# Self- and cross-attention of a decoder layer merged into one program section, with per-batch normalizations on VectorE and GpSimd

## The chip, the cores and the metric

The kernel runs on one core of a Trainium2 chip. The metric is the time of one launch in device microseconds (us), the median of several. TensorE (PE in the rows), VectorE (DVE), ScalarE (ACT), GpSimd (POOL) and SyncE (SP, here only DMA issues) have instruction streams of their own, tied together by semaphores.

## The reference, cut to what matters

B = 8 batches of S = 256 tokens, D = 128, everything in float32. Each sublayer's output is added to its input and normalized without gain or bias.

```python
x = layernorm(x + self_attention(x))             # 16 heads of 8, causal
x = layernorm(x + cross_attention(context, x))   # see below
x = layernorm(x + experts(x))                    # 8 experts of 256, top 2, and a shared one

# cross_attention(context [8, 512, 128], latents = x):
xn, ln = layer_norm(context, g1, b1), layer_norm(latents, g2, b2)
q = ln @ Wq                                      # 16 heads of 64
k, v = split(concatenate([xn, ln]) @ Wkv)        # 768 keys
out = softmax(mask(q k^T / 8)) v @ Wout
```

So the latents are normalized twice between the two attentions: once as the layer's residual, once more with g2 and b2.

## The kernel before, in words

A tile is 128 rows of 128 columns: a batch has 2 tiles of state (`T`), 4 of context (`CT`), together 6 (`KT`). `decoder_layer` calls six stages one after the other, and each is an `nc.Block`, at whose end all engines wait for one another:

```python
self_attention(...)                                 # L311
normalize("n1", ..., whole=True, again=True)        # L207
cross_attention(...)                                # L714
normalize("n2", ...)
experts(...)                                        # L1049
normalize("n3", ..., out=out)
```

**Order of work.** In the attentions and in the experts each engine's stream comes from a table (`Order`, L46): for every kind of step a count per batch and the place of the first, in units of a batch (self-attention 16 heads, cross-attention 32 units of one head and 128 queries, experts 9). A place outside of the batch's own window, such as -4 or 37.75, puts the step among the steps of the batch before or after: the software pipeline. Windows -1, 0, 7 and 8 are written out, windows 1 to 6 are a hardware loop, unrolled by 2 in the attentions (3 turns). `Turns` (L82) deals out PSUM slots in that order and says whose reader has to be done.

**Self-attention**, per batch: projections K, Q, V in three fp32r products (high and low halves); per head POOL makes `q_head` (L469), PE the scores, DVE the masked scores and row minimum (L590), ACT the exponential (L516), PE the transposes (L675), DVE or ACT their copies, PE P times V (L693); per four heads PE spreads the sums (`R`, L701), ACT copies them (L528), DVE divides (`NORM`, L613); at the end PE multiplies by Wo (`OUT`, L708) and DVE adds x. Its step STATS takes bn_stats of the batch's 4 context tiles (L623) and 2 state tiles (L626). SP loads the whole context, 2 MB, into `ctx_all` (L424) near the start, and at about 163 us the experts' weights, 3.3 MB. POOL splits the cross weights into halves (L476, L478).

**n1.** DVE turns the bn_stats of all 48 tiles into mean and 1/sqrt(variance) (a chain of small operations with Sqrt on ACT, table load L289), DVE and ACT normalize the 16 state tiles (L271, L295), DVE takes their bn_stats and goes through the chain a second time.

**Cross-attention**, per batch: DVE normalizes 6 tiles into `normed` (NORMED, L891) and makes the mask rows `bar` (L896); PE transposes (TX for the 2 state tiles, TC for the 4 of context, L976), ACT applies gain and bias into `y` (L839), DVE rounds it to `y_hi` (Y, L901), POOL subtracts to `y_lo` (Y, L819); from these PE makes Q (L990), K (L983) and V; DVE and POOL split K into two halves per head (HI, L907, and LO, L815) and DVE doubles q (TWICE, L921); PE makes scores (S, L1011), DVE masks (L931), ACT takes exponentials (L864, table load at the same line), PE transposes (L1017) and multiplies by V (L1028). Places in the tables of before: TX -26, TC -23 on PE; NORMED -26.75, BAR -26, Y -19 on DVE; Y -25, LO -17.5, WIDE -9.25 on POOL.

**n2, experts, n3.** n2 is as the first half of n1 on the state tiles alone. In the experts the last step of each batch takes bn_stats of the state (L1197); n3 then does the chain (L241 to L258, L289) and the 16 tiles for all batches, and SP issues the output in four transfers of 256 KB (L307).

Of the kernel before, what the change touches and what calls it, by code (L numbers as in the profile page):

```python
# [25 lines left out]
ALU = mybir.AluOpType  # L26
# [19 lines left out]
class Order:  # L46
# [6 lines left out]
    def __init__(self, batches, units, starts):  # L53
        self.batches = batches
        due = []
        for kind, (count, first) in starts.items():
            for i in range(count):
                at = first + i * units / count
                due.append((at % units, kind, int(-(at // units)), i))
        due.sort(key=lambda d: d[0])  # L60
        self.steps = [d[1:] for d in due]
        assert all(-1 <= rel <= 1 for _, rel, _ in self.steps)

    def window(self, w):
        return [s for s in self.steps if 0 <= w + s[1] < self.batches]

    def run(self, engine, emit, unroll):


        def one(w, value):  # L70
            for kind, rel, i in self.window(w):
                emit(kind, value + rel, (w + rel) % 2, i)
        one(-1, -1)
        one(0, 0)
        with engine.Fori(0, (self.batches - 2) // unroll) as turn:
            for n in range(unroll):
                one(1 + n, turn * unroll + 1 + n)
        one(self.batches - 1, self.batches - 1)
        one(self.batches, self.batches)


class Turns:  # L82
# [3 lines left out]
    def __init__(self, order, kinds, places):  # L86
        self.batches, self.places = order.batches, places
# [4 lines left out]
    def place(self, kind, i):  # L92
        return self.at[kind, i] % self.places
# [27 lines left out]
def decoder_layer(nc, x, ctx, mask, wq, wk, wv, wo, g1, b1, g2, b2, xwq, xwkv, xwout,  # L121
# [28 lines left out]
    with top:  # L150
# [9 lines left out]
        stats = sb(top, "stats", [P, B * KT, 6])  # L160
        mean = sb(top, "mean", [P, B * KT])
        rstd = sb(top, "rstd", [P, B * KT])
        var = sb(top, "var", [P, B * KT])
        tmp = sb(top, "tmp", [P, B * KT])
        gb = sb(top, "gb", [P, 4])
        w_rt = sb(top, "w_rt", [P, E])
        w_up = sb(top, "w_up", [P, 2, NE, HID])
        w_down = sb(top, "w_down", [P, NE, HB, D])
# [6 lines left out]
        ctx_all = sb(cross, "ctx_all", [P, B * CT, D])  # L175
# [18 lines left out]
        m.ctx_all, m.keep_all, m.wk_hi, m.wk_lo, m.wv_hi, m.wv_lo = ctx_all, keep_all, wk_hi, wk_lo, wv_hi, wv_lo  # L194
        m.wq_hi, m.wq_lo, m.wout, m.w_up, m.w_down = wq_hi, wq_lo, wout, w_up, w_down
        m.loaded_up, m.loaded_down = sem("loaded_up"), sem("loaded_down")

        self_attention(nc, sem, sb, ps, m)
        normalize(nc, sem, "n1", B * T, state, stats, mean, rstd, var, tmp, T, CT, KT, whole=True, again=True)
        cross_attention(nc, sem, sb, ps, slot, m)  # L200
        normalize(nc, sem, "n2", B * T, state, stats, mean, rstd, var, tmp, T, CT, KT)
        cross.close()
        experts(nc, sem, sb, ps, slot, m)
        normalize(nc, sem, "n3", B * T, state, stats, mean, rstd, var, tmp, T, CT, KT, out=out)


def normalize(nc, sem, name, tiles, state, stats, mean, rstd, var, tmp, T, CT, KT,  # L207
              whole=False, again=False, out=None):
# [8 lines left out]
    stored = sem(name + "_stored")  # L217
    rows = stats[:, :, :].rearrange("p (b k) s -> p b k s", k=KT)

    def per_tile(a, everything):  # L220
        v = a[:, :].rearrange("p (b k) -> p b k", k=KT)
        return v if everything else v[:, :, CT:KT]

    rounds = [whole] + [False] * again
    with nc.Block() as block:  # L225

        @block.vector
        def _(dve):
# [7 lines left out]
            def moments(everything):  # L236

                st = rows if everything else rows[:, :, CT:KT, :]
                me, ve, mo, vo = (st[:, :, :, i] for i in (1, 2, 4, 5))
                m, v, t = (per_tile(a, everything) for a in (mean, var, tmp))  # L240
                link(dve.tensor_tensor(t, me, mo, ALU.subtract))  # L241
                link(dve.tensor_tensor(t, t, t, ALU.mult))  # L242
                link(dve.tensor_tensor(v, ve, vo, ALU.add))  # L243
                link(dve.tensor_scalar(v, v, 1.0 / P, EPS, ALU.mult, ALU.add))  # L244
                link(dve.tensor_scalar(t, t, 0.25, None, ALU.mult))  # L245
                link(dve.tensor_tensor(m, me, mo, ALU.add))  # L246
                link(dve.tensor_scalar(m, m, 0.5, None, ALU.mult))
                dve.tensor_tensor(v, v, t, ALU.add).then_inc(var_ready, 1)  # L248

            def reciprocal_root(n, everything):  # L250

                v, t, r = (per_tile(a, everything) for a in (var, tmp, rstd))
                dve.wait_ge(std_ready, n)
                link(dve.reciprocal(r, r))  # L254
                link(dve.tensor_tensor(t, r, r, ALU.mult))
                link(dve.tensor_tensor(t, t, v, ALU.mult))  # L256
                link(dve.tensor_scalar(t, t, -0.5, 1.5, ALU.mult, ALU.add))  # L257
                link(dve.tensor_tensor(r, r, t, ALU.mult))  # L258

            def at(i):  # L260
                return (i // T) * KT + CT + i % T

            for n, everything in enumerate(rounds):
                moments(everything)
                reciprocal_root(n + 1, everything)
                if n == 0:
                    t, m, r = (per_tile(a, False) for a in (tmp, mean, rstd))
                    dve.scalar_tensor_tensor(out=t, in0=m, scalar=-1.0, in1=r,  # L268
                                             op0=ALU.mult, op1=ALU.mult).then_inc(bias_ready, 1)
                    for i in range(0, tiles, 2):  # L270
                        last = dve.tensor_scalar(state[:, i, :], state[:, i, :], mean[:, at(i):at(i) + 1],  # L271
                                                 rstd[:, at(i):at(i) + 1], ALU.subtract, ALU.mult)
                        if out is not None or i == tiles - 2:
                            last.then_inc(chain, 1)
                            count[0] += 1
                    dve.wait_ge(chain, count[0])
                    if again:
                        for i in range(0, tiles, 2):
                            dve.bn_stats(stats[:, at(i), :], state[:, i, :])
                        for i in range(1, tiles, 2):  # L280
                            dve.wait_ge(act_tiles, i // 2 + 1)
                            last = dve.bn_stats(stats[:, at(i), :], state[:, i, :])
                        link(last)

        @block.scalar
        def _(act):
            for n, everything in enumerate(rounds):
                act.wait_ge(var_ready, n + 1)
# [22 lines left out]
def self_attention(nc, sem, sb, ps, m):  # L311
# [104 lines left out]
    with nc.Block() as block:  # L416

        @block.sync
        def _(sp):
            for i, w in ((0, m.wq), (2, m.wv), (3, m.wo)):  # L420
                sp.dma_start(raw[:, i, :], w).then_inc(loaded_w, 16)
# [845 lines left out]
```

## Time and profile before

| | us |
|---|---|
| median of 3 runs (lowest, highest) | 1204.02 (1203.21, 1204.50) |
| the profiled execution's own time | 1204.94 |
| its span in the trace | 1203.1 |
| PE busy | 1119.0 (93%) |
| DVE busy | 877.1 (73%) |
| ACT busy | 752.6 (63%) |
| POOL busy | 427.4 (36%) |
| mean granted TensorE clock | 0.972 |

The span runs from the first to the last recorded instruction of the profiled execution; that execution's own time is 1.84 us more than its span. Busy times are the sum of an engine's instructions; a granted clock of 1.0 is TensorE's full speed. The self-attention runs from the start to about 199 us, n1 to about 213, the cross-attention to about 985, then n2, the experts to about 1193, and n3.

### The profile page before, as it was taken

To read this page: it belongs to the slowest core of one execution; us is meant where nothing else is said; L and a number is where in the kernel's file an instruction comes from. 1 tells how busy PE (TensorE), PEld (TensorE's weight loads), DVE (VectorE), ACT (ScalarE), POOL (GpSimd) and SP (SyncE) were. 2 spreads that over 40 slices of the span, in tenths; PEclk is the share of its full clock that TensorE was granted. 3 is DMA by queue.
4 is the path that set the end of the run, shared out by engine and by line. 5 is a ranking of instruction groups with operands and counts; after the bars stand their busy time and mean duration, and the time that the engine had idled before them with its cause. 6 is when DMAs were issued, how large, how long until landed. Compare 5 with 4: busy or idle time off the path is not lost. (4 is left out here: it accounts for less than half of the span.)

```text
span 1203.1 us, 29258 instructions
## 1 busy us (share of the span) xinstructions
PE 1119.0 (93%) x8781; PEld 963.3 (80%) x8781; DVE 877.1 (73%) x2772; ACT 752.6 (63%) x1778; POOL 427.4 (36%) x498
## 2 busy tenths in 40 slices
PE   6989894599999999999999989999999986999996
PEld 5777783578888888878888878888888866999995
DVE  7989897687777878767777767777776755555555
ACT  6999895476666767657766666666675754222222
POOL 4656562344435334334433433433433424000000
PEclk9999998799999999999999999999999996899998
DMA  4000050000000000000000000000000000000001
GB/s 141 7 6 9 5 159 1 1 1 2 1 2 2 1 1 2 2 3 2 2 1 2 1 4 2 1 2 1 1 2 1 2 1 1 1 1 0 0 1 35
DMA packets 11403, 12.31 MB, mean 10 GB/s; under 512 B 1152, under 2 KB 9344, under 8 KB 11136
## 3 DMA queue, kind: packets, MB, share of 16 engines
q1 hardware_dynamic: 10848, 10.43, 2.9%
q8 instruction: 67, 1.10, 0.4%
q14 instruction: 72, 0.59, 0.2%
q10 hardware_dynamic: 416, 0.20, 0.1%
HBM read 9.57 MB, written 1.05 MB: 9 GB/s over the span
## 5 line engine op out<-in xcount | busy, mean ns | idle before, releaser
L815 POOL TENSOR_TENSOR xk_parts<-k_raw,xk_parts 64x768 fp32r<-64x768 f32 x128 | 236.4, 1847 | 441.1 <-DVE xk_parts L907 441.1
L931 DVE CUSTOM_DVE_ANT_0 xmasked<-ps,bar 128x768 f32<-128x768 f32 x256 | 244.0, 953 | 6.0 <-issue 1.6
L864 ACT ACTIVATE xprobs<-xmasked,xlow 128x768 f32<-128x768 f32 x256 | 237.9, 929 | 4.6 <-issue 3.8
L1011 PE MATMUL ps<-xk_parts,xq_parts 128*128 128x512 f32 (+1 forms) x1024 | 232.2, 348 | 4.7 <-DVE xq_parts L912 2.9
L1017 PE MATMUL ps<-ident,xprobs 128*128 128x128 f32 x1536 | 215.5, 276 | 2.0 <-DVE xprobs_t L936 1.1
L1011 PEld LDWEIGHTS ps<-xk_parts,xq_parts 128*128 128x128 f32 x1024 | 174.5, 189 | 28.8 <-DVE xq_parts L912 3.4
L1028 PE MATMUL ps<-xprobs_t,xvals 128*64 128x256 f32 x1536 | 179.9, 383 | 1.1 <-ACT xprobs_t L870 1.1
L1017 PEld LDWEIGHTS ps<-ident,xprobs 128*128 128x128 f32 x1536 | 169.4, 140 | 10.7 <-DVE xprobs_t L936 1.3
L1028 PEld LDWEIGHTS ps<-xprobs_t,xvals 128*64 128x64 f32 x1536 | 104.9, 137 | 57.8 <-issue 10.4
L936 DVE COPY xprobs_t<-ps 128x768 f32<-128x768 f32 x128 | 121.6, 950 | 4.7 <-PE ps L1017 4.5
L112 DVE MEMSET xspare<- 128x1 f32 x256 | 15.1, 59 | 145.4 <-PE ps L1011 110.9
L1128 ACT ACTIVATE silu<-ps 128x512 f32<-128x512 f32 x72 | 42.8, 597 | 123.0 <-PE ps L1230 123.0
L516 ACT ACTIVATE probs<-masked,low 128x128 f32<-128x128 f32 (+1 forms) x256 | 114.0, 453 | 2.6 <-DVE low L590 2.5
L870 ACT ACTIVATE xprobs_t<-ps 128x768 f32<-128x768 f32 x128 | 103.3, 807 | 4.1 <-PE ps L1017 2.6
L1180 DVE TENSOR_TENSOR hidden<-ps,silu 128x512 f32<-128x512 f32 x72 | 49.6, 691 | 75.6 <-ACT silu L1128 75.6
L844 ACT ACTIVATE k_raw<-ps 128x768 f32<-128x768 f32 x64 | 52.0, 812 | 74.2 <-PE ps L985 71.1
L1228 PE MATMUL ps<-cxt_hi,up_hi 128*128 (+1 forms) x288 | 88.7, 308 | 0.0
L469 POOL TENSOR_TENSOR q_head<-q_parts,head_of 128x256 fp32r<-128x256 f32 x128 | 76.1, 614 | 31.7 <-DVE q_parts L580 30.9
L876 ACT ACTIVATE xrsum_t<-ps 128x256 f32<-128x256 f32 x64 | 24.6, 384 | 99.4 <-PE ps L1036 99.4
L1230 PE MATMUL ps<-cxt_hi,up_lo 128*128 (+1 forms) x288 | 83.3, 289 | 0.0
L1229 PE MATMUL ps<-cxt_lo,up_hi 128*128 (+1 forms) x288 | 83.1, 288 | 0.0
L1236 PE MATMUL ps<-w_down,hidden 128*128 128x128 f32 x576 | 77.1, 278 | 4.2 <-DVE hidden L1180 4.2
(182 smaller groups left out, 2391.1 us busy)
## 6 DMA issues: line engine op xcount, KB each, us to landing
w_up<-in_L_ffn_w SPq DMA_DIRECT2D x2, 1024.0 KB, 8.8
raw_kv<-in_L_xattn_Wkv SPq DMA_DIRECT2D x1, 1024.0 KB, 11.7
out<-state SPq DMA_DIRECT2D x4, 256.0 KB, 2.6
x_in<-in_x SPq DMA_DIRECT2D x7, 128.0 KB, 2.2
raw_q<-in_L_xattn_Wq SPq DMA_DIRECT2D x1, 512.0 KB, 7.7
wout<-in_L_xattn_Wout SPq DMA_DIRECT2D x1, 512.0 KB, 3.8
keep_all<-in_mask_BxS_bk SPq DMA_DIRECT2D x1, 512.0 KB, 5.7
w_up<-in_L_ffn_sw SPq DMA_DIRECT2D x2, 128.0 KB, 6.9
```

The source lines that it names most:

```text
L516: nc.scalar.activation(probs[:, i % 4, lo:hi], masked[:, r, lo:hi], ACT.Exp, scale=-1.0, bias=low[:, r, j:j + 1], accum_out=sums[:, g % 2, ...
L815: pool.tensor_tensor(k_parts[dst, i // 2 % 2, h, :], k_raw[src, :], k_parts[src, i // 2 % 2, h, :].bitcast(F32), ALU.subtract).then_inc(k_ ...
L864: nc.scalar.activation(probs[:, i % 4, :], masked[:, i % 4, :], ACT.Exp, scale=-1.0, bias=low[:, i % 4:i % 4 + 1], accum_out=sums[:, pair ...
L870: nc.scalar.activation(probs_t[:, i % 4, :, 0, :], slot(slots.place("PT", 2 * i), KEYS).rearrange("p (k t) -> p k t", k=KT), ACT.Copy).the ...
L931: dve.tensor_tensor_reduce(masked[:, i % 4, :], slot(slots.place("S", i), KEYS), bar[:, par, :], 1.0, 3e38, ALU.add, ALU.min, low[:, i % 4 ...
L936: dve.tensor_copy(probs_t[:, i % 4, :, 1, :], slot(slots.place("PT", 2 * i + 1), KEYS).rearrange("p (k t) -> p k t", k=KT)).then_inc(pt_dv ...
L1011: last = nc.tensor.matmul(slot(s, hi - lo, lo), q_parts[:, pair % 2, h, part, t * P:(t + 1) * P], k_parts[:, pair % 2, h, lo:hi], start=pa ...
L1017: last = nc.tensor.transpose(slot(s, P, j * P), probs[:, i % 4, j * P:(j + 1) * P], ident[:, :])
L1028: last = nc.tensor.matmul(ps[h * XD:(h + 1) * XD, O_BANK + i % 2, 0:S], vals[:, i // 2 % 2, j, c:c + XD], probs_t[:, (2 * i + h) % 4, j, : ...
L1228: nc.tensor.matmul(o, wh, xh, start=True, stop=False)
L1229: nc.tensor.matmul(o, wh, xl, start=False, stop=False)
L1230: last = nc.tensor.matmul(o, wl, xh, start=False, stop=True)
```

## The change

1. Both attentions stand in one `nc.Block`. `self_attention` and `cross_attention` now return emit functions per engine. `Order.run` takes `between`, steps of the cross-attention's first batch to be inserted at given places of the self-attention's last windows, and `done`, the kinds not to be issued again; `apart=2` lets the self-attention's loop cover windows 1 to 4 only (2 turns) and writes out 5 and 6.
2. n1 is gone. Per batch the cross-attention does it itself: DVE STATS (6 bn_stats), POOL N1 (12 operations on 128x2, the inverse root by `ALU.pow` and one Newton step, seven waits on its own results), DVE NORM1 (normalizes the 2 state tiles, bn_stats of the result), POOL N2 (the same 12 on 128x6), DVE NORMED one tile at a time. STATS leaves the self-attention but for batch 0.
3. The context comes per batch (256 KB) into a double buffer, the first two loads near the start, the others once `normed` of two batches before is done. The experts' weights are loaded once the self-attention's last batch is added, and memory is laid out anew.
4. n3 is gone: in the experts POOL does the 12 operations per batch, DVE normalizes at place 9 + 2 + 2.25 units, and SP stores each batch (128 KB).
5. n2 stays, without its options.

```diff
-    def run(self, engine, emit, unroll):
+    def run(self, engine, emit, unroll, between=None, done=(), apart=0):
...
-        with engine.Fori(0, (self.batches - 2) // unroll) as turn:
+        with engine.Fori(0, (self.batches - 2 - apart) // unroll) as turn:
             for n in range(unroll):
                 one(1 + n, turn * unroll + 1 + n)
-        one(self.batches - 1, self.batches - 1)
-        one(self.batches, self.batches)
+        for w in range(self.batches - 1 - apart, self.batches + 1):
+            one(w, w)
...
+            @block.gpsimd
+            def _(pool):
+                emit = c.gpsimd(pool)
+                a.gpsimd(pool, {B - 1: steps(emit, "N1", 5, 0, 1) + steps(emit, "N2", 5, 9, 1),
+                                B: steps(emit, "Y", 1, 9, 1)})
+                c.pool_order.run(pool, emit, 2, done=("N1", "N2", "Y"))
...
+                a.scalar(act, {B: steps(emit, "TX", 1, 5, 1) + steps(emit, "TC", 1, 5, 1)})
...
+                a.vector(dve, {B - 2: steps(emit, "STATS", KT, 0, 2),
+                               B - 1: steps(emit, "NORM1", 2, 4, 1) + steps(emit, "NORMED", KT, 13, 0.5),
+                               B: steps(emit, "BAR", 1, 3, 1) + steps(emit, "Y", 1, 7, 1)})
...
+                a.tensor(pe, {B: steps(emit, "TX", 1, 4, 1) + steps(emit, "TC", 1, 4, 1)})
...
         "R": (PAIRS, 5.25), "PV": (PAIRS, 5), "PT": (UNITS, 0.75), "OUT": (1, 37.75),
-        "TC": (1, -23), "TX": (1, -26)})
+        "TC": (1, -13), "TX": (1, -14.5)})
...
-        "NORM": (PAIRS, 9.25), "PT": (UNITS // 2, 2.25), "OUT": (1, 38.5), "NORMED": (1, -26.75),
-        "BAR": (1, -26), "Y": (1, -19), "TWICE": (XH, -5)})
+        "NORM": (PAIRS, 9.25), "PT": (UNITS // 2, 2.25), "OUT": (1, 38.5), "NORMED": (KT, -17.5, 0.5),
+        "BAR": (1, -26), "Y": (1, -11), "TWICE": (XH, -5),
+        "STATS": (KT, -32, 0.75), "NORM1": (2, -23.5, 0.75)})
...
-        "LO": (XH, -17.5), "WIDE": (PAIRS, -9.25), "Y": (1, -25)})
+        "LO": (XH, -5.5), "WIDE": (PAIRS, 2.75), "Y": (1, -13), "N1": (5, -30.5, 1), "N2": (5, -24.5, 1)})
...
+            if group == 2:
+                pool.wait_ge(link, b * LINKS + 3)
+                pool.tensor_tensor(root, var, half, ALU.pow).then_inc(link, 1)
...
+            if kind == "NORM1" and i == 0:
+                dve.wait_ge(scaled1, b + 1)
...
+            if kind == "NORM1" and i == 1:
+                dve.wait_ge(half_renewed, T * (b + 1))
+                dve.memset(early.spare[:, :], 0.0)
...
+                    dve.wait_ge(scaled2, b + 1)
...
+                if kind == "Y" and i == NE - 1:
+                    wait(dve, scaled, b)
+                if kind == "NORM":
+                    dve.wait_ge(scaled, b + 1)
```

**How the order moves.** First PE, from the end of the self-attention's last window to the cross-attention's first Q; `heads_t` and `wo_t` are the self-attention's, `y_hi` the cross-attention's. Before:

```order
L675 MATMUL ps<-ident,probs 128x128 x6
L693 MATMUL ps<-probs_t,vals 32x256 x4
L693 MATMUL ps<-probs_t,vals 32x128 x4
L701 MATMUL ps<-ident,rsum_wide 128x128 x2
L708 MATMUL ps<-wo_t,heads_t 128x128 x8
L416 UNCONDITIONAL_BRANCH
L963 UNCONDITIONAL_BRANCH
L976 MATMUL ps<-ident,normed 128x128 x6
L990 MATMUL ps<-y_hi,wq_hi 128x256
```

And now:

```order
L647 MATMUL ps<-ident,probs 128x128 x6
L1043 MATMUL ps<-ident,normed 128x128 x6
L665 MATMUL ps<-probs_t,vals 32x256 x4
L665 MATMUL ps<-probs_t,vals 32x128 x4
L673 MATMUL ps<-ident,rsum_wide 128x128 x2
L680 MATMUL ps<-wo_t,heads_t 128x128 x8
L1060 MATMUL ps<-y_hi,wq_hi 128x256
```

The two branches, the block's end and the next one's start, are gone, and the transposes of `normed` stand ahead of the last P times V. DVE now, in the same window:

```order
L578 COPY probs_t<-ps 128x384 x2
L587 RECIPROCAL rsum<-sums 128x8
L594 TENSOR_TENSOR heads_t<-ps,rsum_t 128x256
L959 MEMSET bar 128x2x256
L961 TENSOR_SCALAR bar<-keep_all 128x512
L578 COPY probs_t<-ps 128x384
L594 TENSOR_TENSOR heads_t<-ps,rsum_t 128x256
L966 CAST y_hi<-y 128x768
L598 TENSOR_TENSOR state<-ps,x_in 128x256
```

Two mask operations stand ahead of the last copy of transposed probabilities, and the rounding of `y` ahead of the last addition. Third, POOL now, in the window before that one, where nothing stood between `q_head`, `rsum_wide` and the weight splits:

```order
L814 TENSOR_TENSOR x_gap<-xstats 128x6
L815 TENSOR_TENSOR x_var<-xstats 128x6
L816 TENSOR_TENSOR x_total<-xstats 128x6
L452 TENSOR_TENSOR q_head<-q_parts,head_of 128x256
L819 TENSOR_TENSOR x_fix<-x_gap 128x6
L820 TENSOR_SCALAR x_var<-x_var 128x6
L821 TENSOR_SCALAR x_mean<-x_total 128x6
L823 TENSOR_TENSOR x_var<-x_var,x_fix 128x6
L452 TENSOR_TENSOR q_head<-q_parts,head_of 128x256
L467 TENSOR_TENSOR rsum_wide<-ones,rsum 128x256
L826 TENSOR_TENSOR x_root<-x_var,x_powers 128x6
```

The chain N2 now lies between the `q_head` of the last batch, on which PE's scores wait; N1 lies the same way ahead of it. In the cross-attention the same two chains lie between the LO steps.

## Rows read from the trace of the kernel before

**Rows 1.** Windows: start:end, length, each engine's busy (x instructions), PEclk, DMA share, GB/s
```profile
162.77:184.41 21.64, 20.97 (x202) 17.63 (x201) 20.58 (x117) 21.08 (x86) 13.86 (x26) 1.00 0.69 214
210.00:230.00 20.00, 9.26 (x40) 7.87 (x41) 10.01 (x33) 4.92 (x10) 5.62 (x3) 0.63 0.00 1
400.00:600.00 200.00, 197.11 (x1471) 164.93 (x1468) 150.71 (x388) 132.54 (x253) 77.91 (x68) 0.99 0.01 2
1100.00:1160.00 60.00, 60.00 (x518) 60.00 (x517) 32.49 (x84) 15.53 (x26) 0.00 (x0) 1.00 0.00 0
```
**Rows 2.** Timeline, self-attention: start us, us, engine line, out<-in xcount [idle before <-releaser]
```profile
47.43 0.38 ACT L528 ACTIVATE rsum_t<-ps 128x256 f32<-128x256 f32 x1 [0.36 <-PE ps L701]
...
69.27 0.38 ACT L528 ACTIVATE rsum_t<-ps 128x256 f32<-128x256 f32 x1 [0.36 <-PE ps L701]
...
81.74 0.06 DVE L112 MEMSET spare<- 128x1 f32 x1 [3.03 <-issue]
...
93.91 0.38 ACT L528 ACTIVATE rsum_t<-ps 128x256 f32<-128x256 f32 x1 [0.36 <-PE ps L701]
...
140.93 0.39 ACT L528 ACTIVATE rsum_t<-ps 128x256 f32<-128x256 f32 x1 [0.36 <-PE ps L701]
```
**Rows 3.** Timeline, the context half of one batch's STATS on DVE
```profile
186.76 0.86 DVE L623 BATCH_NORM_STATS2 stats<-ctx_all 128x6 f32<-128x128 f32 x4
```
**Rows 4.** Timeline, from the self-attention's end to the first Q
```profile
196.61 2.02 PE L708 MATMUL ps<-wo_t,heads_t 128*128 128x128 f32 x16 [1.02 <-DVE heads_t L613]
...
213.50 0.48 DVE L881 MEMSET bar<- 128x512 f32 x1 [0.67 <-PEq L225]
...
213.90 0.93 DVE L891 TENSOR_SCALAR normed<-ctx_all,mean,rstd 128x128 f32<-128x128 f32 x4
...
214.74 0.59 DVE L891 TENSOR_SCALAR normed<-state,mean,rstd 128x128 f32<-128x128 f32 x2
...
215.25 0.42 DVE L896 TENSOR_SCALAR bar<-keep_all 128x512 f32<-128x512 uint8 x1
...
216.12 0.56 ACT L839 ACTIVATE y<-ps,gb 128x256 f32<-128x256 f32 x1 [4.42 <-PE ps L976]
...
217.78 0.56 DVE L901 CAST y_hi<-y 128x768 fp32r<-128x768 f32 x1 [2.11 <-ACT y L839]
...
218.42 1.80 POOL L819 TENSOR_TENSOR y_lo<-y,y_hi 128x768 fp32r<-128x768 f32 x1 [24.36 <-DVE y_hi L901]
...
220.37 0.55 PE L990 MATMUL ps<-y_hi,wq_hi 128*128 128x256 f32 x1 [3.43 <-POOL y_lo L819]
```
**Rows 5.** Timeline, the filling of the cross-attention
```profile
221.14 0.63 PE L983 MATMUL ps<-y_hi,wk_hi 128*128 128x512 f32 x1
...
227.15 0.96 PE L1011 MATMUL ps<-xk_parts,xq_parts 128*128 128x512 f32 x4 [1.70 <-DVE xq_parts L912]
...
227.95 0.40 PE L983 MATMUL ps<-y_hi,wk_hi 128*128 128x512 f32 x1
...
230.49 1.28 ACT L864 ACT_TABLE_LOAD   x1
```
**Rows 6.** Groups by line: POOL's LO, count, busy us, mean ns, idle before
```profile
L815 POOL TENSOR_TENSOR xk_parts<-k_raw,xk_parts 64x768 fp32r<-64x768 f32 x128 | 236.4, 1847 | 441.1 <-DVE xk_parts L907 441.1
```
**Rows 7.** By source line: count, ns min/median/max, first and last start, forms
```profile
L921 DVE CAST xq_parts<-xq_parts x128: 419/422/1349, 222.7 to 969.0; 64x512 fp32r<-64x512 f32 x128
...
L469 POOL TENSOR_TENSOR q_head<-q_parts,head_of x128: 612/614/620, 11.4 to 186.1; 128x256 fp32r<-128x256 f32 x128
...
L826 POOL TENSOR_TENSOR xrsum_wide<-ones,xrsum x128: 392/401/623, 243.6 to 986.2; 128x128 f32<-128x128 f32 x128
...
L1103 POOL MEMSET index<- x8: 127/128/134, 1004.4 to 1004.7; 128x16 f32 x8
```
**Rows 8.** Timeline, the end
```profile
1192.53 0.49 DVE L1197 BATCH_NORM_STATS2 stats<-state 128x6 f32<-128x128 f32 x2
...
1197.60 2.67 SPq L307 DMA_DIRECT2D out<-state  x4
```

More of the change, by code:

```diff
@@ L92, in place @@
     def place(self, kind, i):
-        return self.at[kind, i] % self.places
+        return (self.at[kind, i] + self.shift) % self.places
     def before(self, kind, batch, i):
@@ L199, in decoder_layer @@
[L199 to L202, printed above, removed]
+        m.loaded_rest, m.loaded_ctx = sem("loaded_rest"), sem("loaded_ctx")
+        m.cross_hi, m.cross_lo = sem("cross_hi"), sem("cross_lo")
+        m.self_added = sem("self_added")
+        early = cross_early(cross, sb, m)
@@ L216, in normalize @@
     act_tiles = sem(name + "_act_tiles")
[L217 to L224, printed above, removed]
+    me, ve, mo, vo = (stats[:, :, i] for i in (1, 2, 4, 5))
+    m, v, t, r = (a[:, :] for a in (mean, var, tmp, rstd))
     with nc.Block() as block:
@@ L234, in link @@
                 dve.wait_ge(chain, count[0])
[L236 to L248, printed above, removed]
@@ L263, in _ @@
[L263 to L283, printed above, removed]
@@ L298, in normalize @@
-        if out is not None:
-            @block.sync
-            def _(sp):
-                rows_out = out.rearrange("b (j p) d -> p (b j) d", p=P)
-                step = 2 * T
-                for i in range(0, tiles, step):
-                    sp.wait_ge(chain, 12 + (i + step) // 2)
-                    sp.wait_ge(act_tiles, (i + step) // 2)
-                    sp.dma_start(rows_out[:, i:i + step, :], state[:, i:i + step, :]).then_inc(stored, 16)
-                sp.wait_ge(stored, 16 * (tiles // step))
@@ L311, in self_attention @@
-def self_attention(nc, sem, sb, ps, m):
+            act.wait_ge(var_ready, 1)
+            nc.scalar.activation(r, v, ACT.Sqrt).then_inc(std_ready, 1)
+            act.wait_ge(bias_ready, 1)
+            for i in range(1, tiles, 2):
+                nc.scalar.activation(state[:, i, :], state[:, i, :], ACT.Identity, scale=rstd[:, i:i + 1],
+                                     bias=tmp[:, i:i + 1]).then_inc(act_tiles, 1)
+def self_attention(nc, sem, sb, ps, m, mem):
     B, S, D, T, C, CT, KT = m.B, m.S, m.D, m.T, m.C, m.CT, m.KT
@@ new lines, in emit @@
+            if kind == "Y":
+                dve.wait_ge(yc_ready, b + 1)
+                dve.wait_ge(yx_ready, b + 1)
+                dve.tensor_copy(y_hi[:, par, :], y[:, :]).then_inc(yh_done, 1)
+            if kind == "HI":
+                n, h = b * XH + i, i % 2
+                rows = slice(h * XD, (h + 1) * XD)
+                dve.wait_ge(k_out, b * PAIRS + i // 2 + 1)
+                wait(dve, full["S"], 2 * n - 6)
+                dve.tensor_copy(k_parts[rows, i // 2 % 2, h, :], k_raw[rows, :]).then_inc(kh_done, 1)
@@ new lines, in emit @@
+            if kind == "NORM":
+                n = b * PAIRS + i
+                dve.wait_ge(rsum_t_ready, n + 1)
+                dve.wait_ge(pv_done, n + 1)
+                if i == 0:
+                    wait(dve, full["OUT"], b)
+                dve.tensor_tensor(heads_t[:, i, :], ps[:, O_BANK + i % 2, 0:S], rsum_t[:, i % 2, :],
+                                  ALU.mult).then_inc(heads_ready, 1)
+            if kind == "OUT":
+                dve.wait_ge(full["OUT"], b + 1)
+                tokens = state[:, bass.ds(b * T, T), :]
+                dve.tensor_tensor(tokens, slot(slots.place("OUT", 0), T * D).rearrange("p (t d) -> p t d", t=T), tokens,
+                                  ALU.add).then_inc(added, 1)
+                dve.wait_ge(added, b + 1)
+                for j in range(T):
+                    last = dve.bn_stats(stats[:, bass.ds(b * T + j, 1), :], state[:, bass.ds(b * T + j, 1), :])
+                last.then_inc(measured, 1)
```

1302 lines of the change are left out of this document (716 added, 586 removed).

## The prediction

> **What bounds the kernel now.** I read the windows view first, stretch by stretch, since a busy share over the whole span mixes stages. In the cross-attention's steady part PE is busy 197.11 of 200 us, DVE 75%, POOL 39% [rows 1]. In the experts PE is busy 60.00 of 60 us. In both, only less or faster PE work would count, and the change takes none away. In the self-attention's last full window PE, DVE and ACT are all within 1.1 us of the window's 21.64, ACT closest with 21.08; POOL has 7.8 us free. The one stretch where nobody is full is the way from the first attention to the second: PE's last self product starts at 196.61 and lasts 2.02, and the first Q starts at 220.37 [rows 4]. That is 21.7 us without PE work but six transposes, and then comes a start at a granted clock of 0.63 [rows 1]. A smaller one lies at the very end. These two are what the change can shorten.
>
> **1. The self-attention's loop.** The same step of consecutive batches is 21.84 us apart within a turn (47.43 to 69.27), 24.64 across a turn's end (to 93.91), and the next two intervals, of which one holds a turn's end, take 47.02 together (to 140.93) [rows 2]. An end of a turn costs 24.64 - 21.84 = 2.8 and 47.02 - 2 x 21.84 = 3.3. DVE's memset at 81.74 shows how: 3.03 us idle, released by nothing but issue. Three turns have two such ends, two turns one: **-3.1**. Ends: -3.3, and 0 if the written-out windows pay the same for being fetched. I take the mean of the two, because a window written out today runs at 21.64 [rows 1]. The removed STATS of seven batches (0.86 for four tiles [rows 3], 0.49 for two [rows 8]) gives nothing, since ACT, which has the fewest idle microseconds, is its cover.
>
> **2. The two windows that now carry batch 0's normalization.** Window 162.77 to 184.41 gets NORM1 (two normalizations at 0.59 a pair [rows 4], two bn_stats at 0.49 [rows 8], a memset: 1.1) and NORMED (0.93 + 0.59 = 1.5 [rows 4]) and loses 1.35 of STATS: DVE goes from 20.58 to about 21.9, just over the 21.64 of the window. POOL gets 24 small operations among the `q_head` on which the scores wait. No trace shows such an operation. A memset of 16 columns took 0.127, a product of 128 columns 0.401, one of 256 columns 0.614 [rows 7]; the line through the last two ends at 0.19 for no columns, and I take that, as the operations are of the kind of these two. From one result to a dependent start elsewhere passes 0.08 (y_hi ends 218.34, y_lo starts 218.42 [rows 4]). A chain is then 12 x 0.19 + 8 x 0.08 = 2.9 us, between 2.2 (0.127 each) and 5.5 (0.401 each). Two chains, 5.8 us, fit into POOL's 7.8 idle ones, but shift some scores: **+1.0**, between 0 and +4 (two chains at 0.401 are 11, 3.2 beyond the idle time).
>
> **3. The join.** What goes is all from OUT's end, 198.63, to Q at 220.37. What is left: memset and mask (0.48 + 0.42 = 0.9 [rows 4]) now stand ahead of DVE's last copy of probabilities, behind which PE's last P times V, the division and OUT are queued. On PE the context's transposes wait for ACT's copy of the state's (0.56, with the transposes themselves about 0.95), beside the same 0.9. So OUT moves by +0.9, to 199.5. The last division is followed on DVE by y_hi (0.56) and on POOL by y_lo (1.80), while PE does OUT (2.02): 0.08 + 0.56 + 0.08 + 1.80 = 2.5, 0.5 more than OUT. Q starts at about 198.63 + 0.9 + 0.5 = 200.0 in place of 220.37: **-20.3**. Ends: -21, if mask and transposes hide wholly, and -18, if y (ACT) or the addition comes late.
>
> **4. The filling.** From Q to the first scores passed 227.15 - 220.37 = 6.8 us, with K's first product at 0.63 where the same took 0.40 seven microseconds later [rows 5]. PE comes out of busy work now, so its part of these 6.8 us runs at full speed: I estimate -1.4. ACT's table load at 230.49 (1.28 [rows 5]) stood ahead of the first exponential; both attentions use Exp and no Sqrt lies between now: -1.2. **-2.6** together, between -3 and 0 (0 if DVE and POOL, not PE, pace the filling). The Trainium skill, "ScalarE: Activation LUTs", section "What ACT_TABLE_LOAD costs", puts a switch of tables at 2.66 us, load and drain; by it this term would be 1.4 larger and the time 1.4 lower. The row shows 1.28 and no drain beside it.
>
> **5. The cross-attention's steady part.** A batch takes about 94 us (127 steps of L921 in 746.3 us, 16 to a batch [rows 7]). DVE gets about 3.1 us (STATS and NORM1), 3% on 75%; POOL gets 5.8, 6% on 39%. PE's work is the same. LO, on which the scores wait, finds POOL idle for 441.1 / 128 = 3.4 us on average ahead of it [rows 6]; the largest piece of a chain between two LO is four operations, about 1.0, so it fits. NORMED, Y and the transposes stand 9 to 12 units closer to their use; Y at -11 and TX at -14.5 are still some 4 units of 2.9 us, over 10 us, ahead of the first Q at -7.25. **+0.5** for seven batches, between -2 and +8 (1.1 us a batch, the largest piece once unhidden).
>
> **6.** n2 is untouched: 0. In the experts' main part DVE is busy 54% and POOL not at all [rows 1]; 3.25 units of 60 / 26 = 2.3 us (ACT's 26 instructions are one a unit [rows 1]), 7.5 us, lie between a batch's last sum and its normalization, where the chain takes 2.9: 0. The transfers: the context per batch has a batch's time. The experts' 3.3 MB moved to about 199 us, free of any reader until the experts; cover is the whole cross-attention, over 700 us.
>
> **7. The end.** From the last bn_stats (1193.02) to the span's end, 1203.1, are 10.1 us: chain with a table load, sixteen tiles, and four transfers, the last issued at 1200.27 and landed 2.8 later [rows 8]. Now: memset 0.15, chain 2.9, DVE two tiles 0.6 and 0.1 of waits, issue 0.1, landing 2.8: 6.7. **-3.4**, between -5.6 (0.127 for each operation, and half the landing time for half the bytes) and -0.9 (0.401 for each).
>
> **Sum:** -3.1 + 1.0 - 20.3 - 2.6 + 0.5 - 3.4 = -27.9. The span goes from 1203.1 to 1175.2; the execution's own time stands 1.84 above its span, 1177.0; that execution was 0.9 above the median of 1204.0, so I predict a median of **1176.1**.
>
> **Rivals.**
> *A, slower: pow.* POOL's `pow` has no row of any kind. Let a call cost P. In N1 and N2 it stands alone between two LO; after an LO's start the next may start 1.85 + 3.4 = 5.3 us later [rows 6] without holding the scores, so a call over 5.3 - 1.85 = 3.4 holds PE by the excess. P = 6 would cost 2.6 in 14 calls, 36; batch 0's two, among the `q_head`, 12 less the 2.0 idle us that the chains left, 10; and the end 6: 1176.1 + 52 = 1228, slower than before. It turns slower at P of about 4.6 (1.2 x 14 + 7 + 4.6 = 28). For it: the operation is a function, not a sum. Against: six columns are few, and 0.40 is what 128 columns of a product cost. Chance 0.04.
>
> *B: the last windows of the self-attention overrun, or the filling collides.* DVE at 21.9 of 21.64 and POOL's chains ahead of `q_head`: if N1 ends late, NORM1 holds DVE and with it the masks of the scores; I price it as term 2 at +4 and term 3 at -18, and term 4 at 0: 1176.1 + 3 + 2.3 + 2.6 = 1184. Chance 0.2.
>
> *C: DVE and POOL hold each other.* One doubling of q took 1.349 where its median is 0.422 [rows 7], as LO ran beside it; all 128 `q_head` lie within 0.612 to 0.620, so POOL isn't the one held. The change adds to each batch eight DVE operations of such a form, and POOL's load grows from 39% to 45%. If every second one is held by half an LO, that is 8 x 0.5 x 0.92 = 3.7 us of DVE per batch, which its 25% idle time covers in the middle; in term 2 it adds 1.5, and where they stand ahead of masks maybe 0.5 a batch: 1176.1 + 1.5 + 3.5 = 1181. The Trainium skill, "SBUF — State Buffer", section "Who interferes with whom", has the rule: the pair of ports that VectorE and GpSimd share is an exclusive lock, and the loser fully blocks. It speaks against moving chains to POOL; the 1.349 agrees with it. Chance 0.15.
>
> *D: the loop's gain isn't there*, since written-out code has to be fetched as well: term 1 at 0, 1179.2. Chance 0.2.
>
> *E: the change gives nothing*, because the steady part loses what the join gives: +28 over seven batches, 4 us each. PE at 98.6% has no such reserve shown against it, but nothing in the rows asks for 4 us. Chance 0.02 for within 0.2% (2.4 us, about what a measurement of this kernel can tell from no change).
>
> **How the numbers follow.** The forecast as it stands gets 0.39. Cases B to D lie between 1179 and 1184, and B with C near 1189; smaller prices (the end at 0.127 an operation gives -0.8, the join at -21 gives -0.7, the table's other end -0.4, the loop's -0.2, the steady part's -2) reach down to about 1171. The range is 1171 to 1189: beyond it lie A, E, and what several misfortunes at once would make, together below 0.2. Faster by over 0.2%: 0.93. Within: 0.02. Slower: 0.05, which is A and 0.01 of B for a stall in the steady part of over 4 us a batch.
>
> **What would show it.** Term 1: only one gap of about 3 us in DVE's timeline in the self-attention, and its last `OUT` product at about 195 instead of 196.6 (with +1.0 and +0.9). Term 3: under 1.5 us between that product's end and the first Q. Term 4: no table load there, K's first product at 0.40, 5.4 us or less from Q to the scores. Term 5: batch to batch the same 94 us, LO's idle time lower by about 0.7 each, and PE still at 98%. Terms 2 and 7: POOL's small operations at 0.19, and 6.7 us from the last bn_stats to the end. Wrong would be: `pow` over 1 us, PE's waits on LO's result in every batch, a window of over 24 us before the join, or a granted clock below 0.9 from the join to the scores.

## The result and the profile after

The changed kernel takes 1189.58 us (median of 5, 1188.23 to 1194.88), the kernel before in the same runs 1203.59: ratio 0.9885, 95% interval 0.987 to 0.990. That is 14 us faster, where 28 were forecast, and just outside the range. A second set of runs beside the experiments gave 1191.19 and 0.9887 (0.9870 to 0.9903). I read the changed kernel's rows from that second set: its profiled execution (1190.69, span 1188.8) is within 0.5 us of that set's median, while the first one's (1194.88) was the slowest of its five.

First the windows of the changed kernel (columns as in [rows 1]), one of the self-attention's late windows and the steady part:

```profile
162.00:184.00 22.00, 19.79 (x188) 15.90 (x180) 19.37 (x107) 19.48 (x79) 17.91 (x42) 1.00 0.01 2
400.00:600.00 200.00, 195.19 (x1452) 161.26 (x1449) 152.71 (x403) 129.56 (x248) 91.20 (x115) 0.99 0.02 4
```

PE did 197.11 us of work in this stretch before and does 195.19 now, with 1452 matmuls in place of 1471 [rows 1]: in the steady part the kernel became slower. In the self-attention's window POOL went from 13.86 busy to 17.91. The timeline of the changed kernel at the join, at the first exponential, and at the end:

```profile
195.23 0.55 DVE L966 CAST y_hi<-y 128x768 fp32r<-128x768 f32 x1
195.46 2.02 PE L680 MATMUL ps<-wo_t,heads_t 128*128 128x128 f32 x16 [1.02 <-DVE heads_t L594]
195.93 1.80 POOL L864 TENSOR_TENSOR y_lo<-y,y_hi 128x768 fp32r<-128x768 f32 x1 [4.12 <-DVE y_hi L966]
198.00 0.39 PE L1060 MATMUL ps<-y_hi,wq_hi 128*128 128x256 f32 x1 [0.52 <-DVE state L598]
...
207.56 0.93 ACT L909 ACTIVATE xprobs<-xmasked,xlow 128x768 f32<-128x768 f32 x1
...
1181.82 0.48 DVE L1355 BATCH_NORM_STATS2 n_stats<-state 128x6 f32<-128x128 f32 x2
1182.38 0.20 POOL L1236 TENSOR_TENSOR n_gap<-n_stats 128x2 f32<-128x2 f32 x1 [15.07 <-DVE n_stats L1355]
1184.05 0.72 POOL L1246 TENSOR_TENSOR n_root<-n_var,n_consts 128x2 f32<-128x2 f32 x1
1185.91 0.60 DVE L1329 TENSOR_SCALAR state<-state,n_mean,n_root 128x128 f32<-128x128 f32 x2 [3.61 <-POOL n_root L1254]
```

And the kernel before, timeline, at its first exponential and at four of the additions that end a batch (538 to 632 lies within a loop turn, 632 to 730 holds a turn's end):

```profile
231.78 0.94 ACT L864 ACTIVATE xprobs<-xmasked,xlow 128x768 f32<-128x768 f32 x1
...
538.45 0.42 DVE L955 TENSOR_TENSOR state<-ps,state 128x256 f32 x1 [2.33 <-PE ps L1043]
...
632.75 0.42 DVE L955 TENSOR_TENSOR state<-ps,state 128x256 f32 x1 [2.34 <-PE ps L1043]
...
730.97 0.42 DVE L955 TENSOR_TENSOR state<-ps,state 128x256 f32 x1 [2.34 <-PE ps L1043]
...
996.33 0.42 DVE L955 TENSOR_TENSOR state<-ps,state 128x256 f32<-128x256 f32 x1 [3.99 <-PE ps L1043]
```

The changed kernel, the same view:

```profile
520.17 0.42 DVE L1020 TENSOR_TENSOR state<-ps,state 128x256 f32 x1 [2.32 <-PE ps L1113]
...
615.91 0.42 DVE L1020 TENSOR_TENSOR state<-ps,state 128x256 f32 x1 [2.33 <-PE ps L1113]
...
717.92 0.42 DVE L1020 TENSOR_TENSOR state<-ps,state 128x256 f32 x1 [2.32 <-PE ps L1113]
...
986.93 0.42 DVE L1020 TENSOR_TENSOR state<-ps,state 128x256 f32<-128x256 f32 x1 [3.99 <-PE ps L1113]
```

A batch took 632.75 - 538.45 = 94.3 and takes 95.7; one with a turn's end took 98.2 and takes 102.0. From these rows the balance, against the kernel before:

| up to | before | after | gained so far | forecast |
|---|---|---|---|---|
| last self product starts | 196.61 | 195.46 | 1.2 | 1.2 |
| first Q | 220.37 | 198.00 | 22.4 | 22.4 |
| first exponential | 231.78 | 207.56 | 24.2 | 25.0 |
| last batch added | 996.33 | 986.93 | 9.4 | 24.5 |
| end of the span | 1203.1 | 1188.8 | 14.3 | 27.9 |

Up to the first exponential the sum went as forecast, within 0.8; then the cross-attention gives back 14.8 us. Of the last line's 4.9, the end itself is 3.6 (from the last bn_stats to the span's end 10.1 before, 6.5 now). Most of the rest lies in the stretch of n2 and the router, where the granted clock differs from execution to execution, with the same code: an altered kernel before (below, one loop turn) took 15.1 us from the last addition to the experts' first product, as the changed one does, where the profile of before has 18.2. By PE's next wait (6.96 in the changed kernel, 3.72 before) 2.3 of these 3.1 us are given back, and 0.9 is left. The cross-attention ends with its last addition, at 996.33 in the kernel before, and not at about 985.

### The profile page after: what moved, and what is told of

It reads as the page before. It is cut to its first block and busy times, and to the rows that moved or that the text cites. A ratio compares the mean times of both kernels' runs of the same rounds, so it can differ in the third digit from the quotient of the medians.

```text
span 1193.1 us, 29522 instructions
## 1 busy us (share of the span) xinstructions
PE 1126.9 (94%) x8781; PEld 966.4 (81%) x8781; DVE 879.5 (74%) x2763; ACT 740.4 (62%) x1756; POOL 506.4 (42%) x790
## 5 line engine op out<-in xcount | busy, mean ns | idle before, releaser
L1081 PE MATMUL ps<-xk_parts,xq_parts 128*128 128x512 f32 (+1 forms) x1024 | 235.2, 352 | 5.6 <-DVE xq_parts L977 3.4
L1087 PEld LDWEIGHTS ps<-ident,xprobs 128*128 128x128 f32 x1536 | 170.1, 141 | 13.7 <-DVE xlow L996 7.1
L1275 ACT ACTIVATE xvals<-ps 128x512 f32<-128x512 f32 x72 | 42.8, 597 | 123.1 <-PE ps L1388 123.1
L118 DVE MEMSET xspare<- 128x1 f32 x256 | 15.1, 59 | 136.9 <-PE ps L1081 104.3
L1337 DVE TENSOR_TENSOR xvals<-ps,xvals 128x512 f32<-128x512 f32 x72 | 49.6, 691 | 73.0 <-ACT xvals L1275 73.0
L1394 PE MATMUL ps<-w_down,xvals 128*128 128x128 f32 x576 | 77.3, 278 | 4.2 <-DVE xvals L1337 4.2
```

The costliest lines, as they stand in the source:

```text
L1081: last = nc.tensor.matmul(slot(s, hi - lo, lo), q_parts[:, pair % 2, h, part, t * P:(t + 1) * P], k_parts[:, pair % 2, h, lo:hi], start=pa ...
L1087: last = nc.tensor.transpose(slot(s, P, j * P), probs[:, i % 4, j * P:(j + 1) * P], ident[:, :])
L1394: last = nc.tensor.matmul(slot(s, D, j * D), hidden[:, i % 3, k * S + j * P:k * S + (j + 1) * P], w_down[:, i, k, :], start=(k == 0), stop ...
```

## The experiments

Theory 1: PE waits for the PSUM slot of TX and TC until ACT has copied y. The change moved TX and TC next to other users of their slots. Theory 2: DVE's added and moved work delays the masks, on which exponential and transposes hang. Theory 3: POOL's chains hold LO, or hold DVE. The batch period, the time between two batches' first exponentials within a turn, repeats to 0.1 us and tells them apart: 94.3 before, 95.8 after (the additions above give 95.7).

**POOL's chains and DVE's statistics left out.** Both leave out part of the computation, as the expectations say.

```diff
# e2_nochain, in chain(), batches 1 to 7
+            if not (isinstance(b, int) and b == 0):
+                pool.tensor_tensor(gap, me, mo, ALU.subtract).then_inc(link, (1, 2, 1, 2, 1)[group])
...
# e3_nostats, batches 1 to 7: STATS, and likewise NORM1
+                    dve.memset(early.stats[:, i:i + 1, 0:1], 0.0).then_inc(fresh, 1)
```

> Leaves out the moments of batches 1 to 7 in the cross-attention: of each chain of 12 small GpSimd operations 5 or 6 subtractions remain (no power, no Newton step), so these batches use mean and root of batch 0. POOL has some 4 us less per batch. Theory 3 (the chains hold LO or, through the shared port, VectorE): the batch period falls by over 1 us from 95.8. Theories 1 and 2: it stays within 0.3 us, and the total moves by under 2 us.

> Leaves out the bn_stats of batches 1 to 7 and the first of their two normalizations: VectorE's six bn_stats and NORM1 become memsets of one column, about 2.5 us less per batch. Theory 2 (VectorE's added work delays the masks): the batch period falls by about 1 us or more from 95.8. Theories 1 and 3: by under 0.3 us.

Measured: 1191.5 and 1187.0 (one execution each); batch period 95.7 and 95.3. Six of the twelve operations of each chain, the power among them, are worth 0.1 us a batch: at the change's places theory 3 falls for them. The six that remain were not taken out in any run. Six bn_stats and NORM1, 2.5 us of a DVE that idles a quarter of the time, are worth 0.5: a third of the loss.

**Other places for the transposes.**

```diff
# e1_slots, old and new values: PE, then ACT, DVE and POOL
-        "TC": (1, -13), "TX": (1, -14.5)})
+        "TC": (1, -11.5), "TX": (1, -13.5)})
-        "TC": (1, -12.5), "TX": (1, -14)})
+        "TC": (1, -11), "TX": (1, -13)})
-        "Y": (1, -11)
+        "Y": (1, -9.5)
-        "Y": (1, -13)
+        "Y": (1, -11.25)
# e5_phase, the new values: PE, then ACT, DVE and POOL (Y as in the change), and how PSUM slots are dealt out
+        "TC": (1, -15), "TX": (1, -18)})
+        "TC": (1, -14.75), "TX": (1, -18)})
+        "NORMED": (KT, -18.75, 0.01), "NORM1": (2, -25, 0.75)
+        "N2": (5, -25.5, 1)
-    slots = Turns(pe_order, full, SLOTS, 1)
+    slots = Turns(pe_order, full, SLOTS, 2)
# e7_actfirst, ACT alone
-        "TX": (1, -14)
+        "TX": (1, -14.25)
```

> The changed kernel loses 1.4 to 1.5 us in every batch of the cross-attention against the kernel before, in scores 18 to 21 of 32, where the transposes TX and TC now stand; after TX the next user of its PSUM slot is a K product 0.75 units later. Here TX stands at -13.5 and TC at -11.5 on PE (next users of their slots: scores at 19.75, transposes at 20.75), ACT's copies at -13 and -11, Y at -9.5 on DVE and -11.25 on POOL. Theory 1 (K waits for the slot until ACT has copied y): the batch period falls from 95.8 to 94.5 to 95, the median by 5 to 9 us against the changed kernel. Theory 2 (VectorE's added work delays the masks) and theory 3 (POOL's chains): the period stays at 95.5 to 96, the median within 2 us of the changed kernel's 1189.6.

> TX, TC and NORMED stand at the same place within the group of four units, and before the same users of their PSUM slots, as in the kernel before, eight units later: PE TX -18, TC -15, ACT -18 and -14.75, NORMED grouped at -18.75, NORM1 -25, N2 -25.5, Y as in the change. Theory 1 (a transpose costs what the next user of its slot waits for ACT's copy of y): the batch period falls from 95.8 to 94.6 to 95.0 (before: 94.3, and STATS keeps its 0.3), the median by 5 to 9 us against the changed kernel. Theory 2 (VectorE's added work as such): it stays at 95.5 or more; the grouped NORMED would even add 0.7 as in the run before.

> ACT copies the state's transposes into y ahead of the exponential of the same unit, not behind it (place -14.25 in place of -14). Theory 1: K's wait for the slot, 0.5 us at each batch's score 19, goes down to 0.1 or less, but the exponential behind it comes 0.55 later: period 95.3 to 96. Theory 2: K's wait isn't a term of its own, period 95.8 within 0.1.

`e1_slots` missed: 1206.73 us, no faster than the kernel before (ratio 1.0005, 0.9993 to 1.0016), batch period 97.7. The cause is the one of theory 1, in a worse place. Its timeline, two waits in one batch (idle before, and releaser, in brackets):

```profile
664.38 0.96 PE L1081 MATMUL ps<-xk_parts,xq_parts 128*128 128x512 f32 x4 [0.40 <-ACT y L884]
...
669.54 0.66 PE L1087 MATMUL ps<-ident,xprobs 128*128 128x128 f32 x4 [0.95 <-ACT y L884]
```

Scores and transposes now stand behind the slots, and they feed the masks and exponentials at once, where K has slack behind it. I had gone by the distance to the next user alone. The same view of the unaltered changed kernel shows K behind ACT's copy:

```profile
649.05 0.93 ACT L909 ACTIVATE xprobs<-xmasked,xlow 128x768 f32<-128x768 f32 x1
...
649.97 0.56 ACT L884 ACTIVATE y<-ps,gb 128x256 f32<-128x256 f32 x1
650.58 0.50 PE L1053 MATMUL ps<-y_hi,wk_hi 128*128 128x512 f32 x1 [0.27 <-ACT y L884]
```

The copy stands behind an exponential of 0.93. `e7_actfirst` turns the two round; K's wait is gone, the period 95.2 (0.6 less), the time 1186.1 (one execution). `e5_phase` missed as well: 1190.26 (ratio 0.9877, 0.9860 to 0.9893), period 95.6. K no longer waits for y, and the wait behind NORMED at score 16 is gone, but the grouped NORMED and NORM1 stand where other masks follow: PE now waits 0.35 at score 8 and 0.16 at score 18, and the gain goes into that. So neither theory stands alone: each place costs by what waits right behind it.

**Other places for DVE's steps.**

```diff
# e4_grouped
-        "NORMED": (KT, -17.5, 0.5)
+        "NORMED": (KT, -17.5, 0.01)
# e8_holes, the new values
+        "NORMED": (KT, -17.8, 0.01), "STATS": (KT, -29.8, 0.005), "NORM1": (2, -21.8, 0.01)
+        "N1": (5, -30.8, 0.8), "N2": (5, -23, 0.8)
```

> NORMED's six normalizations stand together at place -17.5 on VectorE, in place of one each half unit. In the changed kernel scores 18 and 19 lose 0.3 to 0.4 us each just there. Theory 2: grouped, they hold one mask by 1.5 us in place of several by 0.3; the period changes by over 0.3 us either way. Theory 1: the period stays within 0.3 us of 95.8.

> The changed kernel with VectorE's added steps put where VectorE idles 2.3 us waiting for the scores, once in four units, just ahead of the masks at places 2.25, 6.25, ...: STATS grouped at -29.8, NORM1 at -21.8, NORMED grouped at -17.8; POOL's N1 at -30.8 and N2 at -23, each step 0.8. Transposes as in the change. Theory 2a (a normalization costs PE what it delays the mask behind it, not its own length): the two stalls of 0.37 (score 4) and 0.45 (score 16) go, the batch period falls from 95.8 to 94.9 to 95.2, the median by 4 to 6 us. If the amount of VectorE work is what counts, it stays at 95.5 to 96.5 (grouping it elsewhere gave 96.5).

`e4_grouped`: 1194.5 (one execution), period 96.5, 0.7 more: the work is the same, the place another. `e8_holes` missed: STATS behaved as expected (no stall at score 4), but the kernel became slower than the changed one, 1199.68 (ratio 0.9943, 0.9926 to 0.9960), period 97.0. Its timeline, DVE and POOL:

```profile
630.54 2.20 DVE L940 TENSOR_SCALAR state<-state,x_mean,x_root  x2
630.59 1.82 POOL L860 TENSOR_TENSOR xk_parts<-k_raw,xk_parts 64x768 fp32r<-64x768 f32 x1 [2.31 <-DVE xk_parts L972]
...
643.17 2.70 DVE L954 TENSOR_SCALAR normed<-ctx_in,x_mean,x_root 128x128 f32<-128x128 f32 x4 [1.10 <-POOL x_root L836]
643.19 1.82 POOL L860 TENSOR_TENSOR xk_parts<-k_raw,xk_parts 64x768 fp32r<-64x768 f32 x1 [0.16 <-POOL x_root L836]
```

Two normalizations that take 0.59 together [rows 4] take 2.20, four that take 0.93 take 2.70, both times with LO's 1.82 beside the first of them, which alone takes 1.95 and 1.93. By source line the longest NORMED operation is 1931 ns in this kernel and 506 in the last one below:

```profile
L954 DVE TENSOR_SCALAR normed<-ctx_in,x_mean,x_root x32: 297/335/1931, 185.2 to 844.6; 128x128 f32<-128x128 f32 x32
```

And in `e11_best`, described below:

```profile
L954 DVE TENSOR_SCALAR normed<-ctx_in,x_mean,x_root x32: 298/342/506, 181.7 to 819.8; 128x128 f32<-128x128 f32 x32
```

That is rival C, at a place where it hurts. The 1.10 ahead of 643.17 is a second cost: N2 ended late, DVE waited for it, masks behind.

**The ends of the loop's turns.** In `e6_unroll` all four engines of the cross-attention run with one turn; `e10_before_unroll` does this to the kernel before and nothing else.

```diff
-                c.pe_order.run(pe, emit, 2, done=("TX", "TC"))
+                c.pe_order.run(pe, emit, 2, done=("TX", "TC"), apart=4)
```

> The changed kernel again, unaltered, beside the three that follow, to have a profile of an execution near its median (the one at hand took 1194.9 against a median of 1189.6). Both theories: median 1188 to 1191, batch period inside a loop turn 95.8 again, to 0.1; what differs from the first profile is where TensorE's clock was granted at half speed.

> The cross-attention's loop makes one turn in place of three, windows 3 to 8 are written out. If the pause at a turn's end is the jump back (a stall of some 3 us on issue, and after it a stretch at half clock), both go: the two long periods of 100.4 to 102.3 fall to about 96, the total by 9 to 12 us against the changed kernel. If written-out code has to be fetched at the same price (rival D of the prediction), the periods stay at 100 or spread, the total within 2 us.

> The kernel before with nothing changed but the cross-attention's loop: one turn in place of three. If the pause at a turn's end is the jump's and not the change's, the two long periods of 98.9 and 98.2 fall to 94.3 to 94.6, the total by 7 to 9 us against the kernel before (1203.6 to 1204.6).

`e0_after`: 1191.19, period 95.8. `e6_unroll`: 1180.15 (ratio 0.9798, 0.9781 to 0.9814), 11.0 less, periods 95.5 to 95.9 throughout; the two periods with a turn's end, 100.7 and 102.0, were 11.1 over two plain ones. `e10_before_unroll`: 1194.25 (0.9907, 0.9890 to 0.9923) against 1205.71 beside it, 11.5 less where 7 to 9 were expected, periods 93.8 to 94.2. The turn ends of the kernel before, 98.9 and 98.2, were only 8.5 over two plain periods; some 2 us more came because the plain periods shrank from 94.3 as well, and no run shows why. Writing out the windows is thus worth 11 us to either kernel, though in the kernel before not all of it at the turn ends. PE's timeline at such an end, first of the kernel before:

```profile
514.39 0.38 PE L1001 MATMUL ps<-wv_hi,y_hi 128*128 128x256 f32 x1 [2.89 <-issue]
```

After:

```profile
495.76 0.38 PE L1071 MATMUL ps<-wv_hi,y_hi 128*128 128x256 f32 x1 [3.17 <-issue]
```

The pause itself is 3 us. A stretch at a granted clock of 0.5 follows at the two ends of the changed kernel (3.41 and 6.83 us long) and at the first of the two before, not at its second, where PE paused 3.11 us. How the rest of each end's cost divides between the clock and a pipeline that has to close up again is not shown.

**What helps, together.**

```diff
# e9_all: e8_holes, e7_actfirst and e6_unroll, and the self-attention with one turn
-        pe_order.run(pe, emit, 2, between, apart=2)
+        pe_order.run(pe, emit, 2, between, apart=4)
# e11_best: e9_all with NORMED (KT, -17.5, 0.5), NORM1 (2, -23.5, 0.75), N2 (5, -24.5, 1) as in the change
```

> All that helped together: the holes of the run before, ACT's copy of the state's transposes ahead of the exponential, both attentions' loops with one turn. Expected as a sum from the changed kernel's 1191.2 in the last comparison: -11 (cross loop), -4 (copy first), -5 (holes), -3 (the self-attention's last end of a turn): 1168, between 1165 and 1173. All batch periods between 94.2 and 95.

> Both loops with one turn, ACT's copy first, STATS grouped in VectorE's idle time at -29.8 with N1 at -30.8; NORM1, NORMED and N2 at the places of the change, since the run with all of them moved had a VectorE normalization of 1.95 us beside GpSimd's LO. If that hold was the reason, the batch periods are 94.7 to 95.0 (95.2 of the copy-first run less 0.3 to 0.4 for STATS) in place of 95.9, and the median is 1177.2 less 7 x 1.0, 1169 to 1171.5. If the reason was another (one turn in both loops, or the copy), it stays at 1175 to 1178.

`e9_all`: 1177.23 (0.9760, 0.9744 to 0.9776), outside its 1165 to 1173, periods 96: the holds of `e8_holes` are in it. `e11_best`: **1169.07** (median of 5; ratio 0.9698, 0.9685 to 0.9712), periods 94.7 to 95.0, as its expectation had it. It is 36 us faster than the kernel before. Its steady part:

```profile
400.00:600.00 200.00, 198.84 (x1500) 165.69 (x1499) 159.07 (x418) 135.26 (x258) 97.35 (x126) 1.00 0.01 4
```

1500 matmuls where the kernel before had 1471, with DVE at 80%.

## Why the prediction was right or wrong

**Term 1, the self-attention's loop (-3.1):** right for the turn's end, and too small by what I set at zero, STATS. Rows of the changed kernel that answer to [rows 2]:

```profile
68.63 0.39 ACT L510 ACTIVATE rsum_t<-ps 128x256 f32<-128x256 f32 x1 [0.36 <-PE ps L673]
92.89 0.38 ACT L510 ACTIVATE rsum_t<-ps 128x256 f32<-128x256 f32 x1 [0.35 <-PE ps L673]
135.96 0.39 ACT L510 ACTIVATE rsum_t<-ps 128x256 f32<-128x256 f32 x1 [0.35 <-PE ps L673]
157.68 0.39 ACT L510 ACTIVATE rsum_t<-ps 128x256 f32<-128x256 f32 x1 [0.36 <-PE ps L673]
181.31 0.38 ACT L510 ACTIVATE rsum_t<-ps 128x256 f32<-128x256 f32 x1 [1.03 <-PE ps L673]
```

At 135.96 it is 4.97 us ahead of the 140.93 before: one end of a turn, and 0.3 us a batch (21.54 in place of 21.84) that came with STATS gone. STATS is the only step taken out of these windows, but no run puts it back. ACT was not the cover I took it for. Rival D fell here, and by the two one-turn kernels everywhere: written-out code pays no such pause.

**Term 2 (+1.0)** was right in kind, and a third of what it turned out. The first window with batch 0's steps took 181.31 - 157.68 = 23.63, 2.0 more than a plain one. From there to the last product passed 195.46 - 181.31 = 14.15, where the kernel before took 196.61 - 184.41 = 12.20 (184.41 is the same step there): 1.95 more, of which term 3 had forecast 0.9. That makes 3.0 for term 2. Term 1 gave 5.1 by 157.68 in place of 3.1. The two errors cancel, and the last product came 1.2 us earlier, as forecast: luck, and not a confirmation.

**Term 3 (-20.3)** was right to 0.1 for what lies between the last product and Q. OUT's end to Q is 0.52, but what released Q is the addition to the state, not y_lo, which ends at 197.73; that the 0.5 came out is luck too.

**Term 4 (-2.6)** measured -1.8. From Q to the first scores passed 203.33 - 198.00 = 5.3 in place of 6.8, which is the forecast's -1.4, at a granted clock of 0.98. The second half is where it erred: from the scores to the first exponential 4.2 passed in place of 4.6, 0.4 less where I had given 1.2 to the table load. The timeline of the kernel before shows that the load hardly held the exponential:

```profile
231.40 0.08 DVE L931 DVE_READ_ACCUMULATOR2_ANT xlow<- 128x1 f32 x1
```

The row minimum, which the exponential needs, was ready at 231.48, and the load of [rows 5] ended at 231.77: it cost 0.3 us, not 1.28. And in the changed kernel a stretch at half clock lies behind the start of the scores (0.63 for K's product at 204.74, as before the change).

**Term 7 (-3.4)** was right in its sum: 6.5 us for 6.7. The small operations took 0.20, where the intercept of two rows gave 0.19, but the power took 0.72, and the chain 3.5 (1182.38 to 1185.88) in place of 2.9; from the store's issue at 1186.54 to the end passed 2.3 in place of 2.9, and the two errors cancel. **Rival A** did not come, though `pow` over 1 us, which I had named as a sign of being wrong, did: with two columns it takes 0.71, with six 1.35 (in single cases 1.83), under the 3.4 from which it would have held LO.

**Term 5 (+0.5) is the step that failed;** it measured +14.8 by the balance, outside its bounds of -2 to +8. It went: +1.4 to +1.5 in each of seven batches, some 10 us (95.8 against 94.3); +1.0 in the last; the rest, some 3.6, at the ends of turns and in the first batch, where the half-clock stretches lie otherwise than before. Within a batch PE has three new stalls, read in the fifth batch as what the time between two starts has over the usual time of the same pair: 0.37 at score 4 (a mask behind STATS), 0.45 at score 16 (behind NORMED) and 0.51 at score 19 (K behind ACT's y). Another 0.2 lies in two pieces within the scores at 643.48. Their sum is 1.5; the kernel before has none over 0.13. The first two in the timeline of the changed kernel, DVE and PE:

```profile
602.76 0.29 DVE L935 BATCH_NORM_STATS2 xstats<-state 128x6 f32 x1
602.98 0.95 DVE L996 CUSTOM_DVE_ANT_0 xmasked<-ps,bar 128x768 f32<-128x768 f32 x1
603.99 0.88 PE L1087 MATMUL ps<-ident,xprobs 128*128 128x128 f32 x6 [0.21 <-DVE xlow L996]
...
639.53 0.57 DVE L954 TENSOR_SCALAR normed<-ctx_in,x_mean,x_root 128x128 f32<-128x128 f32 x2
640.60 0.95 DVE L996 CUSTOM_DVE_ANT_0 xmasked<-ps,bar 128x768 f32<-128x768 f32 x1
641.62 0.88 PE L1087 MATMUL ps<-ident,xprobs 128*128 128x128 f32 x6 [0.29 <-DVE xlow L996]
```

The third is shown by `e7_actfirst` (0.6): it has the other two and not this one. The first is shown by `e3_nostats` and `e11_best`, where it is gone. The second moves with NORMED (`e4_grouped`: 0.7 more a batch; `e5_phase`: gone from score 16), but no run has it without another in its place; the 0.2 is located only.

Two sentences of the prediction carried the error. "3% on 75%" and "DVE ... 25% idle time covers": the idle time is not spread out. The waits of DVE ahead of a mask in the changed kernel are one of 1.3 to 2.3 us every four units and at most 0.6 between, and an instruction elsewhere delays the mask behind it. And "PE's work is the same" for the transposes, where I priced only how far they moved from their use, not what stands next in their slots and ahead of ACT's copy. **Rival C** was read rightly from the 1.349 of [rows 7]. At the change's own places it stayed small: q's doubling has a median of 423 ns and a mean of 481, and the chains cost 0.1 a batch. `e8_holes` shows its full price.

The trace of before could not show a price for term 5 by itself, as the places were new. I took that for a small price; the wide end of its range, +8, would have given 1183.6, still short of the measured 1189.58, so the range was too narrow as well.

## What to carry to other kernels

When an engine is saturated and its feeders idle a fraction of the time, find where in the period they idle, and price each inserted step by what stands behind it there: here 2.5 us of VectorE work cost 0.5 us a batch, and moving six normalizations by under three units added 0.7. When a step that fills a shared PSUM slot is moved, name the slot's next user and what ACT does before it frees the slot: swapping one copy with one exponential gave 0.6 us of 95.8. And a pause on issue at the end of each turn costs more than its 3 us: in the changed kernel the two ends cost 4.9 and 6.2 us, and writing out the windows gained 11 us in either kernel, where the change gained 14.

## What I had not expected of the hardware

Half-clock stretches mostly follow a pause of PE of 2 us or more, but not every such pause has one (the 3.11 us at 704.7 in the kernel before has none), and they differ between executions of the same kernel: the changed kernel's two profiles have 23.9 and 13.7 us of them before 800 us, and lie 4.3 us apart in span.

A VectorE normalization of 128x128 went from 0.34 to 1.93 us when GpSimd's 1.82 us subtraction ran beside it; GpSimd's own time stayed at 1.82. The Trainium skill, "SBUF — State Buffer", section "Who interferes with whom", says that a `tensor_scalar` in a two-port mode contends with GpSimd, and that whichever issues first has the shared ports for its whole instruction while the other is blocked. The rows agree that the one waits for the whole of the other: in `e8_holes` each held normalization ends 0.08 to 0.09 us after LO does. They also show how near the two cases lie. The held ones start between 0.05 us before and 0.15 us after LO; in the changed kernel normalizations that start 0.15 to 0.22 us before LO take their plain 0.33.
